# A graph network megakernel: adjacency turned inside the projection, mixing inside the steps, norms inside the stages that make the rows

## What is computed

```python
h = jnp.maximum(_layernorm(x, axis=-1), 0.0)
x = x + _L0_gnn_ref(h, adj, ...)   # graph attention, 16 heads, then hidden @ W_out + b_out and elu
h = jnp.maximum(_layernorm(x, axis=-1), 0.0)
x = x + _L1_gnn_ref(h, adj, ...)   # two steps of top-p mixing, then a layer norm with gamma and beta
h = jnp.maximum(_layernorm(x, axis=-1), 0.0)
x = x + _L2_gnn_ref(h, adj, ...)   # graph attention, 8 heads, elu, then four dense layers
h = jnp.maximum(_layernorm(x, axis=-1), 0.0)
x = x + _L3_gnn_ref(h, adj, ...)   # sparse attention over given pairs, 8 heads
```

```python
for s in range(STEPS):                       # 2 steps
    A = _adj_from_feats(Xa, W1, W2, W3)      # softmax(Xa W1 W2 (Xa W3)^T), cut to the top 0.9 of each row
    Xf = R @ Xf
    Xa = A @ Xa
    Z = Z + (Xf @ U1s[s] + Xa @ U2s[s])
Y = X + Z
```

## Time and profile before

| what | value |
|---|---|
| median of three runs | 4621.47 us (4621.46 to 4624.59) |
| the profiled execution | 4627.39 us, its span 4625.3 us |
| busy: TensorE, VectorE | 3600.6 us (78%), 3656.5 us (79%) |
| busy: ScalarE, GpSimd | 2520.6 us (54%), 1393.1 us (30%) |
| granted TensorE clock, mean | 0.883 of full speed |
| moved | 239.8 MB, mean 52 GB/s |

### The profile page before, as it was taken

The page is one execution under the profiler, slowest core; times in us unless marked ns, Lnnn a source line. Parts: engine busy times, 40 slices in busy tenths (PEclk is TensorE's granted clock), DMA queues, the critical chain, the costliest instruction groups (busy, mean ns, idle before and its releaser), DMA issues. The chain is left out here.

```text
span 4625.3 us, 57062 instructions
## 1 busy us (share of the span) xinstructions
PE 3600.6 (78%) x20004; PEld 2088.3 (45%) x20004; DVE 3656.5 (79%) x6017; ACT 2520.6 (54%) x2957; POOL 1393.1 (30%) x1400
## 2 busy tenths in 40 slices
PE   4897888959997447899874475898887687888887
PEld 3587888624443123344432232576663332333333
DVE  4499999679999984499999845698884329999986
ACT  3366556348998872299898711354442234444442
POOL 0344100006997981179989700000000000000000
PEclk9998899979998769999997797999998897888888
DMA  5411000221210002411100044000001311111110
GB/s 191 160 44 28 25 30 20 76 74 46 58 39 21 7 5 90 131 44 41 39 14 7 6 142 146 20 17 15 18 10 32 127 68 39 41 57 41 46 41 14
DMA packets 162771, 239.81 MB, mean 52 GB/s; under 512 B 86225, under 2 KB 95328, under 8 KB 156784
## 3 DMA queue, kind: packets, MB, share of 16 engines
q1 hardware_dynamic: 149808, 197.90, 13.2%
q0 software_dynamic: 12656, 37.95, 2.2%
HBM read 170.30 MB, written 65.43 MB: 51 GB/s over the span
## 5 line engine op out<-in xcount | busy, mean ns | idle before, releaser
L1392 DVE SCALAR_TENSOR_TENSOR junk<-expd,mid 128x2048 bf16<-128x2048 f32 x440 | 1036.1, 2355 | 14.0
L516 ACT ACTIVATE steepz<-s1b,thr_h 128x1024 bf16<-128x1024 f32 (+1 forms) x768 | 665.6, 926 | 553.6 <-DVE mask L599 473.1
L659 PE MATMUL acc<-V,mask 128*128 128x198 bf16 (+1 forms) x5504 | 757.8, 277 | 192.0 <-DVE mask L601 192.0
L659 PEld LDWEIGHTS acc<-V,mask 128*128 128x128 bf16 x5504 | 487.1, 100 | 252.8 <-DVE mask L601 152.1
L1294 ACT ACTIVATE junk_s<-expd,nmid 128x2048 bf16<-128x2048 f32 x264 | 528.4, 2001 | 102.2 <-POOL nmid L1352 93.9
L1297 ACT ACTIVATE junk_s<-expd,nmid 128x2048 bf16<-128x2048 f32 x264 | 528.1, 2000 | 0.0
L1733 PE MATMUL psS<-KT,qs 64*128 64x512 f32 x1024 | 383.2, 740 | 156.7 <-DVE m L1843 152.2
L666 PE MATMUL acc<-V,adjT 128*128 128x99 bf16 (+1 forms) x5504 | 455.7, 221 | 0.0
L599 DVE TENSOR_TENSOR mask<-steepz,adjT 128x1024 bf16<-128x1024 bf16 (+1 forms) x768 | 397.6, 552 | 29.4 <-PE acc L659 14.9
L666 PEld LDWEIGHTS acc<-V,adjT 128*128 128x128 bf16 x5504 | 371.4, 100 | 51.5 <-issue 3.3
L1336 POOL TENSOR_SCALAR part<-signs,nmid 128x1 f32<-128x1 f32 x264 | 309.2, 1171 | 167.8 <-ACT junk_s L1297 147.1
(11 more groups left out here) (260 smaller groups left out, 5876.7 us busy)
## 6 DMA issues: line engine op xcount, KB each, us to landing
rows<-in_adj_dram SPq DMA_DIRECT2D x32, 1024.0 KB
s1b<-sT_dram SPq DMA_DIRECT2D x32, 512.0 KB, 4.1
block<-adj_dram SPq DMA_DIRECT2D x32, 512.0 KB, 4.4
adj_dram<-adjT POOLq DMA_DIRECT2D x4, 2048.0 KB, 20.5
rel_table<-zeros POOLq DMA_DIRECT2D x64, 128.0 KB, 19.8
y_dram<-yo SPq DMA_DIRECT2D x32, 256.0 KB, 2.1
yt<-y_dram SPq DMA_DIRECT2D x32, 256.0 KB, 2.9
adjT<-adj_dram SPq DMA_DIRECT2D x4, 2048.0 KB
```

The lines of the kernel that those rows point to most:

```text
L516: act.activation(steepz[:, m % RELUS, :], s1b[:, q % 4, :], ACT.Relu, bias=thr_h[:, u, 1, j:j + 1], scale=STEEP).then_inc(relu_ready, 1)
L659: mm = pe.matmul(acc[:, c % 2, i // TB, o:o + 2 * W], mask[:, j % RING, tile(i)], V[:, u, j, 0:2, :].rearrange("p s w -> p (s w)"), start= ...
L1392: link(dve.scalar_tensor_tensor(junk[:, :], e, col(mid, i), e, ALU.is_gt, ALU.mult, accum_out=col(mass, i)))
```

## The change

`adjacency_stage` is gone. Its loads, conversions and transposes stand in the first `project_stage`, a row block after each product tile; 13 of the loads are issued ahead of the transfers of scores, three behind them. Three of the four `norm_stage` calls are gone too: a class `RowNorm` makes the statistics in groups of four tiles as soon as a tile of new rows is there, and scale, ReLU and turn follow, inside `elu_out_stage`, the last `mix_stage` and `mlp_stage`. In the last two, GpSimd adds beta or the bias to `xt`. The first `mix_stage` and the projection of step 1 are gone: step 0 turns each result tile (G), makes K and Q of step 1 from it by one folded weight (J) and writes both out; step 1 loads them and adds the U2 product to its weighing, with eight weight matmuls in place of four. The steps have six buffers `expd` instead of seven and new orders.

The core of the diff (of the orders two lines stand here; what they change is shown below):

```diff
+ROWS_FIRST = 13
+XO = 8
+LAG = 9
...
-ROW_BLOCKS = 7
+ROW_BLOCKS = 6
 TOP_P_ORDER = (
-    {"kinds": "DADDADDAADDAADDD", "slots": "0123456023514630",
+    {"kinds": "DAADDADDDAADADDD", "slots": "0123450340123542",
...
+class RowNorm:
...
+    def moments(self, dve, link, t, src):
+        link(dve.bn_stats(self.stats[:, t, :], src))
...
+            for u in range(t - 3, t + 1):
+                last = dve.bn_aggr(self.mv[:, u, :], self.stats[:, u, :])
+            link(last)
+            dve.tensor_scalar(self.veps[:, t - 3:t + 1], self.mv[:, t - 3:t + 1, 1], LN_EPS, None,
+                              ALU.add).then_inc(self.v_ready, 1)
...
+        act.activation(self.sd[:, 4 * g:4 * g + 4], self.veps[:, 4 * g:4 * g + 4], ACT.Sqrt).then_inc(self.sd_ready, 1)
...
+        link(dve.reciprocal(self.rstd[:, c], self.sd[:, c]))
+        dve.scalar_tensor_tensor(self.nmr[:, c], self.mv[:, c, 0], -1.0, self.rstd[:, c],
+                                 ALU.mult, ALU.mult).then_inc(self.r_ready, 1)
...
+        act.activation(self.nat[:, t, :], src, ACT.Relu, bias=self.nmr[:, t:t + 1],
+                       scale=self.rstd[:, t:t + 1]).then_inc(self.h_ready, 1)
...
+            mm = pe.transpose(self.ps[:, t % 2, k, :], self.nat[:, t, tile(k)], self.b.ident[:, :])
...
+        act.copy(self.tr[:, :, tile(t)], self.ps[:, t % 2, :, :]).then_inc(self.n_copied, 1)
...
-    def adjacency_stage(self):
...
+                def load_rows(t):
+                    if t >= 2:
+                        sp.wait_ge(cast, t - 1)
+                    sp.dma_start(rows[:, t % 2, :], adj_dram[tile(t), :]).then_inc(adj_in[t % 2], 16)
...
+                def turned(t):
+                    for half in range(2):
+                        dve.wait_ge(a_ready, 2 * t + half + 1)
+                        dve.tensor_copy(self.adjT[:, half * NT // 2:(half + 1) * NT // 2, tile(t)],
+                                        psA[:, half, :, :]).then_inc(a_copied, 1)
...
+                        act.activation(rows16[:, t % 2, :], rows[:, t % 2, :], ACT.Copy,
+                                       accum_out=deg[:, t:t + 1]).then_inc(cast, 1)
...
+                def turn_rows(t):
+                    pe.wait_ge(cast, t + 1)
+                    if t == 0:
+                        pe.wait_ge(id_done, 2)
+                    for half in range(2):
+                        if t >= 1:
+                            pe.wait_ge(a_copied, 2 * t + half - 1)
+                        for j in range(NT // 2):
+                            mm = pe.transpose(psA[:, half, j, :], rows16[:, t % 2, tile(half * NT // 2 + j)], ident16[:, :])
+                        mm.then_inc(a_ready, 1)
 
...
+                for t in range(NT + LAG):
+                    if t < NT:
+                        self.transpose_tiles(pe, psT, t, nat, t_ready, t_copied)
+                    if t == 0:
+                        pe.wait_ge(w_in, 16 * (KD + 1))
+                    if 1 <= t <= NT:
+                        u = t - 1
+                        pe.wait_ge(t_copied, u + 1)
+                        if u >= 2:
+                            pe.wait_ge(v_ready, u - 1)
+                        for k in range(KD):
+                            mm = pe.matmul(psO[:, u % 2, :], tr[:, k, tile(u)], w[:, k, :],
+                                           start=(k == 0), stop=(k == KD - 1))
+                        mm.then_inc(o_ready, 1)
+                    if t >= LAG:
...
+                for t in range(NT + LAG + 1):
+                    if t < NT:
+                        act.wait_ge(t_ready, t + 1)
+                        act.copy(tr[:, :, tile(t)], psT[:, t % 2, :, :]).then_inc(t_copied, 1)
+                    if 2 <= t < NT + 2:
+                        u = t - 2
+                        act.wait_ge(neg_ready, u + 1)
+                        act.activation(neg[:, u % 2, :], neg[:, u % 2, :], ACT.Exp).then_inc(exp_ready, 1)
+                    if t >= 7 and (t - 7) % 4 == 0 and (t - 7) // 4 < NT // 4:
+                        norm.root(act, (t - 7) // 4)
+                    if LAG - 1 <= t < NT + LAG - 1:
+                        norm.relu(act, t - LAG + 1, xo[:, (t - LAG + 1) % XO, :])
+                    if t >= LAG + 1:
...
+                    dve.wait_ge(x_ready, t + 1)
+                    norm.moments(dve, link, t, xo[:, t % XO, :])
...
+                        pool.tensor_tensor(xt[:, t % 4, :], xt[:, t % 4, :], b4[:, :], ALU.add).then_inc(b_ready, 1)
...
+                        dve.tensor_tensor(xo[:, t % XO, :], psO[:, t % 2, :], xt[:, t % 4, :], ALU.add).then_inc(x_ready, 1)
+                        dve.wait_ge(x_ready, t + 1)
+                        norm.moments(dve, link, t, xo[:, t % XO, :])
...
+                pe.wait_ge(w1T_copied, 1)
+                for k in range(KD):
+                    mm = pe.matmul(psW[:, 1, k * H:(k + 1) * H], w1T[:, tile(k)], w2[:, :], start=True, stop=True)
+                mm.then_inc(w12_ready, 1)
...
+                if s == 1:
+                    sp.dma_start(KT[kk, :], kq_dram[q, :]).then_inc(kq_in, 16)
+                    sp.dma_start(QT[kk, :], kq_dram[kk, :]).then_inc(kq_in, 16)
+                for n, name in enumerate(("L1_gnn_U1_0",) if s == 0 else ("L1_gnn_U1_1", "L1_gnn_U2_0")):
+                    sp.dma_start(w[:, n * KD:(n + 1) * KD, :], a[name].rearrange("(k p) d -> p k d", p=P)).then_inc(w_in, 16)
+                if s == 1:
+                    for c in range(4):
+                        for j in range(4 * c, 4 * c + 4):
+                            sp.dma_start(parts[:, j, :, :], parts_dram[j]).then_inc(parts_in[c], 16)
+                    for c in range(4):
+                        sp.dma_start(nat[:, 4 * c:4 * c + 4, :],
+                                     xa_dram[4 * c * P:4 * (c + 1) * P, :].rearrange("(t p) d -> p t d", p=P)
+                                     ).then_inc(nat_in[c], 16)
+                n = {c: 0 for c in "apixygj"}
                 for c in order["sp"]:
...
+                        for k in range(KD):
+                            pe.matmul(psX[:, bank["Q", t], :], xT[:, t % 2, k, :], w[:, KD + k, :], start=False, stop=False)
...
+                def turn_result(f):
+                    pe.wait_ge(o_copied, f + 1)
+                    turn(("G", f), [xo[:, f % 2, tile(k)] for k in range(KD)])
+
+                def next_kq(f):
+                    n = group["J", f]
+                    pe.wait_ge(t_copied, max(group["G", f] + 1, n - 1))
+                    for k in range(KD):
+                        mm = pe.matmul(psT[:, n % 2, 0, :], w13n[:, k, :], xT[:, f % 2, k, :],
+                                       start=(k == 0), stop=(k == KD - 1))
+                    mm.then_inc(t_ready, 1)
...
+                        pool.tensor_tensor(xt[:, t % 4, :], xt[:, t % 4, :], bet[:, :], ALU.add).then_inc(b_ready, 1)
...
-            b.adjacency_stage()
...
-        b.norm_stage(xa, natA, trB)
-        b.top_p_stage(natA, trA, natB, trB, step_dram, parts_dram, xa, xb, y_dram)
+        b.elu_out_stage(natB, trA, a["L0_gnn_W_out"], a["L0_gnn_b_out"], a["x"], xa)
...
-            b.norm_stage(xb, natA, trB, adj_in)
+            b.mix_stage(natA, trB, a["L1_gnn_U2_1"], step_dram, y_dram, xa, xb, adj_in)
...
-            b.mlp_stage(natB, trA, xb, xc)
-        b.norm_stage(xc, natA, trB)
+        b.mlp_stage(natB, trA, xb, xc)
```

724 lines of the change are left out of this document (418 added, 306 removed).

## The result

The changed kernel takes 4424.41 us (median of four, 4421.97 to 4426.97) against 4622.82 us before: 198.4 us less, a ratio of 0.957 (95% interval 0.9558 to 0.9582). Forecast were 4438 us, 13.6 us more. The profiled execution has a span of 4420.9 us at a mean clock of 0.896; that of before had 4625.3 at 0.883, so 204.4 us are to be explained between the two traces. That is 6.0 us more than between the medians: the profiled execution of before (4627.39 us) was longer than its median, that of after (4422.61 us) shorter.

What follows compares the result with a forecast made beforehand. VectorE was taken to bound the two top-p steps; loading, engines waiting in turn and barriers the short stages. Terms summed to -183 us from 4627.4, 4444, less 5.9 to the median: 4438 us, range 4398 to 4488.

Steps and rivals of the forecast that it cites:

- Seven terms: Stage forecasts: adjacency -28.7, elu -21, projection of step 0 +3, step 0 +14, step 1 +17, mixing -36, MLP -25 us.
- Adjacency, forecast -28.7: The adjacency stage of 62.65 us goes; its work adds 34.0 us to the first projection.
- Elu, mixing, MLP: These stages, each with its norm fused in beside the products, get shorter by 21, 36 and 25 us.
- drain of 1.38 us at a table switch: ScalarE in elu: by the skill's rule 3.8 us a tile, still under 4.06; about 1.4 us at the tail.
- Step 0, +14: First top-p step: a tail of 41 us adds 18, fewer waits for GpSimd's thresholds take some off.
- three quarters of the waits: In step 0, the share of VectorE's 16.7 us of waits for GpSimd's thresholds taken to go in the new order.
- Step 1, +17: Second top-p step: K and Q loads +4, first adjacency block +2, tail +15, waits for GpSimd -4 us.
- the first adjacency block behind 13.6 MB: At step 1's start VectorE's first block is queued behind other loads, some 38 us with latency, mostly covered: +2 us.
- Six buffers: Rival, 15%: in the steps new tiles' exponentials wait for an older tile's application, three waits, +50 us: 4488 us.
- GpSimd's addition: Rival, 5%: at 4.2 + 0.54 us it bounds the MLP's last loop, 62 us in place of 32.7: 4467 us.
- Slower than before by reuse of buffers: Rival, 2%: each of twenty buffer reuses in the steps waits a whole apply of 16.7 us, +334 us: 4772 us.
- That the steps do not lengthen: Rival, 10%: the longer tails of both steps are paid by waits that go, 31 us less: 4407 us.

Runs made afterwards that it cites:

- u_norms: The changed kernel with the fused norm taken out of the elu, mixing and MLP stages and a norm stage behind each instead: 4515.01 us in one run.
- u_adj: The changed kernel with the adjacency stage of before put back ahead of the first norm, and the first projection without it: 4471.48 us, ratio 0.9669.
- i_loads: The changed kernel with step 1's first adjacency block loaded ahead of the split rows, the second behind them, weights and result rows only then: 4419.39 us.

## Why the prediction came out, and where it did not

*The mechanism was right, and the terms less than their sum.* VectorE is busy as long as before in both steps (724.3 and 696.4 us), and the short stages get shorter where engines no longer wait in turn: u_norms and u_adj give 90.6 and 47 us back when the parts are undone. The stages that the change touches were forecast at -183 and measured at -186. Seven terms are off by 27 us when their misses are added without sign, and by 3 with it, so they largely cancel; that part is luck.

*The step that failed is the silent one*, that a stage which isn't touched costs what it cost. The sum had no term for the first attention; it gave 16.3 us, of which 15.4 are the gaps at the loop's turns. With them 4438 would have been 4422 or 4423.

*Adjacency, forecast -28.7, measured -33.4.* The 16 transposes of a row block were priced at 1.89 us from the earlier trace rows. In that stage each of the sixteen groups stood behind a pause and took 1.86 to 1.89. In line behind products fourteen of sixteen take 1.06 or 1.07; the two behind the longest waits take 1.86 and 1.89. One of the two and its successor, in the changed kernel:

```profile
58.77 1.86 PE L462 MATMUL psA<-ident,rows 128*128 128x128 bf16 x16 [3.39 <-DVE adjT L387]
...
65.94 1.06 PE L462 MATMUL psA<-ident,rows 128*128 128x128 bf16 x16
```

```profile
58.70:60.70 2.00, 1.93 (x17) 1.96 (x18) 1.24 (x3) 0.00 (x0) 0.00 (x0) 0.50 0.81 242
65.90:67.00 1.10, 1.10 (x18) 1.05 (x17) 0.41 (x1) 0.85 (x2) 0.00 (x0) 1.00 0.00 0
```

The granted clock is 0.50 and 1.00 of full speed in the two, 1.2 and 2.4 GHz. (the earlier trace rows has 1.00 for the adjacency stage of before, but that trace holds no record of the clock ahead of 88 us, and the view puts 1.00 where it has none. That the stage ran at the low clock is read from the durations alone.) So 16 x 1.89 = 30.2 us was too dear by some 12; pauses of 8.2 us for conversions and copies, put at 1.5, took part of it back.

*Elu, mixing, MLP* (forecast 92, 108.5, 123; measured 91.0, 104.4, 125.6). A tile of the mixing stage takes 4.7 us where 4.92 were counted, since the next transposes begin before the last product's modelled end. In the MLP the loop's products take 33.1 us (32.7), the 2.25 us behind the slow `nmr` among them, the tail behind them 14.2 where 10.3 were counted: ScalarE waits 2.1 us for the last group's statistics before that group's root and ReLUs. The Trainium skill's drain of 1.38 us at a table switch, which the prediction named (ScalarE: Activation LUTs, What ACT_TABLE_LOAD costs), isn't seen; the load of 1.28 us begins 0.02 us behind the instruction before it, and the next one 0.01 us behind the load, in the changed kernel's elu stage:

```profile
847.33 0.63 ACT L819 ACTIVATE neg<-neg 128x512 f32<-128x512 f32 x1 [0.23 <-DVE neg L853]
847.98 1.28 ACT L135 ACT_TABLE_LOAD   x1
849.27 0.20 ACT L135 ACTIVATE sd<-veps 128x4 f32<-128x4 f32 x1
```

*Step 0, +14, measured +8.7.* The last two keeps do not follow one another: the one on VectorE's block is done at 1702.8, that of ScalarE's waits 12.2 us for GpSimd and starts at 1715.17, so three quarters of the first application are over by then. The tail behind the last keep is 31.2 us, not 41. The term "three quarters of the waits" was wrong too: they stay (15.6 us against 16.7 in the earlier trace rows). Waits for peaks at the step's start took 2.1 us more (8.4 against 6.3).

```profile
DVE expd L1608 <- POOL mid L1556: 15.6, 4, 12.2
DVE top L1581 <- PE psL L1331: 8.4, 2, 6.6
```

*Step 1, +17, measured +25.2.* The start took +7.3 us (4 were counted), the peaks that came late +10.4 (2), GpSimd's waits and the tail together +7.6 (11: 28.9 and 31.4 us against 18.6 and 34.1). The mis-sized term is the first adjacency block behind 13.6 MB: it was counted at 2 us, and cost 5.9 at the fourth peak, which i_loads takes away. The other late peak, 4.5 us at 2171, was not foreseen at all, and stays in i_loads. Its logits wait 10.0 us for ScalarE's exponentials of the block before, and those (at 2162.80) stand in ScalarE's order behind a pass of a test that waits for GpSimd until 2160.80:

```profile
2164.89 6.48 PE L1331 MATMUL psL<-KT,B 128*128 128x512 f32 x8 [10.01 <-ACT expd L1429]
```

*The rivals.* Six buffers did not starve VectorE: in the middle of step 0 it waits for no peak, in step 1 twice, for the two causes above. GpSimd's addition takes 1.28 us, not 4.2; what it costs beyond that is the slow `nmr`. Slower than before by reuse of buffers: ScalarE's exponentials wait for an application three times in both steps together, 2.4 us in all, and in the kernel before, with seven buffers, four times, 2.3 us. That the steps do not lengthen is refuted: together they take 33.9 us more.
